# In a unit the next batch's values are projected ahead of the first value products, keys and the seventh product for maxima behind them

## The reference

```
x   = x + tanh(g_xattn) * Attention(layernorm(x), ctx)      # x [8, 56, 128], ctx [8, 1500, 128]
      q = xn @ w_q.T, k = ctx @ w_k.T, v = ctx @ w_v.T      # 16 heads of 8
      softmax(q k^T / sqrt(8)) v, then @ w_o.T
x   = x + tanh(g_ffn) * MoE(layernorm(x))                   # 8 experts, the best 2 of each token
```

## Time and profile before

| | us |
|---|---|
| median of three runs | 282.74 (282.09 to 285.79) |
| the profiled execution's own time | 280.42 |
| its span, from first to last instruction | 278.7 |
| PE busy | 265.4 (95%) |
| DVE busy | 216.7 (78%) |
| ACT busy | 178.6 (64%) |
| POOL busy | 125.2 (45%) |
| granted TensorE clock, mean | 0.999 |

### The profile page before, as it was taken

One profiled execution on the slowest core, in us unless ns is written; L12 is line 12 of the kernel. 1 busy time (PEld: TensorE's weight loads), 2 busy tenths in 40 slices (PEclk: granted clock), 3 DMA queues, 4 the chain that ended last, 5 costly groups with the idle time before them and its releaser, 6 DMA issues.

```text
span 278.7 us, 8055 instructions
## 1 busy us (share of the span) xinstructions
PE 265.4 (95%) x2807; PEld 218.9 (79%) x2807; DVE 216.7 (78%) x460; ACT 178.6 (64%) x369; POOL 125.2 (45%) x148
## 2 busy tenths in 40 slices
PE   7889899999999999999999999996989999999994
PEld 2466688888788888888878887885888789999962
DVE  4679788887977889788887887788466988888771
ACT  2637586687676777678668774465718878776500
POOL 3587852763466266195266310123520855554200
PEclk9999999999999999999999999999999999999999
DMA  7398964972990892695497299300000000000001
GB/s 256 102 205 215 215 154 118 255 187 57 245 237 23 239 240 75 171 238 145 109 243 202 53 214 284 125 0 2 2 2 1 0 0 0 0 5 0 0 0 33
DMA packets 9957, 32.40 MB, mean 116 GB/s; under 512 B 2592, under 2 KB 3104, under 8 KB 9920
## 3 DMA queue, kind: packets, MB, share of 16 engines
q1 hardware_dynamic: 9504, 31.80, 45.0%
q10 hardware_dynamic: 432, 0.33, 0.4%
HBM read 13.26 MB, written 0.23 MB: 48 GB/s over the span
## 4 chain that ended last, share of the span: by engine, by line
PE 74%; ACT 6%; DVE 6%; DMA 6%; SPq 3%; issue 2%; POOL 2%; DVEq 0%; ACTq 0%
PE max_ps L1053 14%; PE o_ps L1074 13%; PE score_ps L1033 13%; PE misc_ps L1012 7%; PE misc_ps L1005 5%; DMA ctx_sb<-in_ctxT 5%; SPq L251 3%; PE score_ps L1269 3%; ACT probs L548 3%; PE score_ps L1271 2%; PE score_ps L1270 2%; PE o_ps L1371 2%; PE o_ps L1269 2%; PE o_ps L1271 2%; PE o_ps L1270 2%
## 5 line engine op out<-in xcount | busy, mean ns | idle before, releaser
L734 DVE TENSOR_REDUCE part_max<-max_ps 112x1 f32<-112x512 f32 (+1 forms) x192 | 117.7, 666 | 28.6 <-PE max_ps L1053 26.8
L548 ACT ACTIVATE probs<-score_ps 128x448 f32<-128x448 f32 x188 | 88.0, 549 | 11.3 <-PE score_ps L1033 11.0
L1053 PE MATMUL max_ps<-kx,qx 96*112 96x512 f32 (+1 forms) x192 | 79.9, 422 | 2.3 <-DVE part_max L734 1.3
L1033 PEld LDWEIGHTS score_ps<-qx,kx 104*128 104x128 f32 x376 | 64.0, 188 | 7.8 <-issue 0.3
L1033 PE MATMUL score_ps<-qx,kx 104*128 104x224 f32 x376 | 67.3, 277 | 0.0
L1074 PE MATMUL o_ps<-probs,v_sb 128*32 128x112 f32 (+1 forms) x1536 | 45.2, 261 | 1.3 <-ACT probs L548 0.8
L1074 PEld LDWEIGHTS o_ps<-probs,v_sb 128*32 128x32 f32 (+1 forms) x1536 | 37.5, 110 | 7.5 <-ACT probs L548 5.1
L1053 PEld LDWEIGHTS max_ps<-kx,qx 96*112 96x112 f32 x192 | 33.7, 177 | 8.3 <-issue 4.6
L542 ACT ACTIVATE v_sb<-misc_ps 128x512 f32<-128x512 f32 x24 | 14.4, 601 | 29.2 <-PE misc_ps L1012 29.2
L370 POOL TENSOR_TENSOR k_low<-k_full,k_high 128x512 fp32r<-128x512 f32 (+1 forms) x21 | 26.3, 1252 | 13.8 <-ACT k_full L530 13.5
L406 POOL CAST ctx_parts<-ctx_sb 128x512 fp32r<-128x512 f32 (+1 forms) x18 | 10.8, 600 | 46.3 <-DMA ctx_sb<-in_ctxT 29.9
(11 more groups left out here) (192 smaller groups left out, 385.4 us busy)
## 6 DMA issues: line engine op xcount, KB each, us to landing
kx<-k_high SPq DMA_DIRECT2D x60, 187.5 KB, 5.3
kx<-k_low SPq DMA_DIRECT2D x30, 187.5 KB, 5.2
ctx_sb<-in_ctxT SPq DMA_DIRECT2D x7, 750.0 KB, 5.8
gu_sb<-in_guT SPq DMA_DIRECT2D x8, 512.0 KB, 5.5
dn_sb<-in_dnT SPq DMA_DIRECT2D x8, 256.0 KB, 5.8
ctx_sb<-in_ctxT SPq DMA_DIRECT2D x2, 256.0 KB, 3.9
kx<-k_high SPq DMA_DIRECT2D x4, 123.5 KB, 2.3
kx<-k_high SPq DMA_DIRECT2D x4, 64.0 KB, 2.0
```

Source lines behind the costliest of these rows:

```text
L548: nc.scalar.activation(probs[:, (KT * h + t) % 8, :], bank[:, 0:SC // 2], ACT.Exp, scale=SCALE).then_inc(exp_done, 1)
L734: nc.vector.reduce_max(part_max[:, p, c:c + 1], max_ps[0:PC, bank, 0:size], AX.X).then_inc(max_taken, turns)
L1033: last = nc.tensor.matmul(bank[0:m, GC * g:GC * g + GC], kx[0:KR, 2 * par + h, g, 128 * t:128 * t + m], qx[0:KR, par, 2 * h + g, :], start ...
L1053: nc.tensor.matmul(max_ps[0:PC, bank, 0:size], qx[0:MR, par, 2 * h + p // 2, PC * (p % 2):PC * (p % 2) + PC], kx[0:MR, slot, p // 2, start ...
```

## The change

Jobs 0 and 1 trade their kinds: job 0 becomes the values job and job 1 the keys job, in the loop's twelve units. The seventh product moves from in front of run 0 to behind it, in the fourteen units that share this code. ACT's order of copies follows. On DVE the wait for the reciprocals' completion moves in front of reductions 4 and 5, and the shuffle in front of the seventh reduction. The jobs at c = 2 stay.

```diff
             def evacuate(i, par, h, c):
                 b = batch(i, par)
-                if c == 1:
+                if c == 0:
                     v_copy(b + 1, 1 - par, 1 + h)
                 elif h == 1 and c == 2:
                     ...
                 else:
-                    if h == 0 and c == 0:
+                    if h == 0 and c == 1:
                         keys_moved(i, par)
                         act.wait_ge(k_low_saved, NCH * (b + 2))
-                    k_copy(b + 2, par, 2 if h else c // 2, misc_ps)
+                    k_copy(b + 2, par, 2 if h else c - 1, misc_ps)
...
                 reciprocals(u - 1, 1 - h)
+                dve.wait_ge(den_taken, u + 1)
                 for n in range(MID, RUN):
                     take_max(ring(u, n), n % 3, AHEAD + n)
-                dve.wait_ge(den_taken, u + 1)
+                spread_inverse(u - 1, 1 - h)
                 take_max(ring(u, SEVENTH), SEVENTH % 3, AHEAD + RUN, turns=2)
-                spread_inverse(u - 1, 1 - h)
...
             def project(i, par, h, c):
-                if h == 0 and c == 0:
-                    pe.wait_ge(v_saved, NCH * (b + 1) + 1)
-                    k_product3(i, par, 0)
+                if c == 0:
+                    if h == 0:
+                        pe.wait_ge(v_saved, NCH * (b + 1) + 1)
+                    else:
+                        pe.wait_ge(k_saved, 2 * (NCH * (b + 2) + 2))
+                    v_project(1 - par, 1 + h)
                 elif c == 1:
-                    pe.wait_ge(k_saved, 2 * (NCH * (b + 2) + 1 + 2 * h))
-                    v_project(1 - par, 1 + h)
+                    pe.wait_ge(v_saved, NCH * (b + 1) + 2 + h)
+                    k_product3(i, par, 2 * h)
                 elif h == 0:
-                    pe.wait_ge(v_saved, NCH * (b + 1) + 2)
+                    pe.wait_ge(k_saved, 2 * (NCH * (b + 2) + 1))
                     k_product3(i, par, 1)
-                elif c == 0:
-                    pe.wait_ge(k_saved, 2 * (NCH * (b + 2) + 2))
-                    k_product3(i, par, 2)
                 else:
-                    pe.wait_ge(v_saved, NCH * (b + 2))
+                    pe.wait_ge(k_saved, 2 * (NCH * (b + 2) + 3))
                     v_project(par, 0)
...
                 job(i, par, h, 0)
+                attend(i, par, h, 0)
                 max_scores(*u1, AHEAD + RUN, ring(u, SEVENTH), SEVENTH % 3, turns=2)
-                attend(i, par, h, 0)
                 job(i, par, h, 1)
```

## The result

| | before | after |
|---|---|---|
| median of 6 runs, us | 283.14 (282.09 to 285.79) | 288.03 (287.80 to 288.72) |
| the profiled execution's own time | 280.42 | 287.91 |
| its span | 278.7 | 286.2 |
| PE busy | 265.4 | 272.9 |
| DVE busy | 216.7 | 231.1 |

A forecast was written before the change was run, and what follows sets the result against it. The prediction took PE's order as the bound, with ACT's copy of job 1 and exponentials 6 to 8 in each unit's chain. ACT's copies +4.5 and the late context -2.5 gave +2.0 us: 284.7 from 282.74, range 279.9 to 288.3.

The forecast's parts named there:

- Run 0's start: On PE, with a values job alone in front, run 0 starts 0.07 (h = 0) and 0.11 us (h = 1) earlier.
- The credit of 0.18 a pair: The earlier starts of run 0 on PE, 0.07 us in h = 0 and 0.11 in h = 1, counted against the loss.
- ACT's copies: Behind job 1 one ACT copy becomes two; exponential 6 comes 0.45 (h = 0) and 0.30 us (h = 1) later, 4.5 in all.
- The doubt that I took from the Trainium skill: Shown matmul ends are computed, so PE's credits could be void: loss 5.7 us, forecast 1.2 higher; the credits were kept.
- The late context: In units of h = 0, ACT's waits for keys 0 caused by a late context go: a gain of 2.5 us.
- DVE: The wait for the reciprocals' completion in front of reductions 4 and 5 costs some 0.15 us a unit, taken as 0.
- this sign of being wrong: A new idle piece, POOL or DVE as releaser, in front of keys 1, product 10 or the transposed maxima.
- POOL: Chunk 1's split, released by keys 0, ends 0.75 us before keys 1 needs it, so it costs 0.
- The POOL rival: Slower case: chunk 1's split becomes the wait; 287.8 us, or 289.0 with the copies' loss at its upper bound; chance 0.10.
- SP: Chunk 2's `k_low` and twelve queued keys transfers come some 1.4 us later, the context goes out 2.3 earlier; cost 0.
- Absorbed: Faster rival: tile 11 does not carry the later exponentials to run 1, only the gain stays, 280.2 us; chance 0.17.

The follow-up runs named there:

- `k_low` late: Changed kernel with POOL's `k_low` of chunk 0 moved behind chunk 2's split; median 285.97 us, 1.0117 of the kernel before.
- run 1: No follow-up run: a step of PE in each unit, behind run 0, job 2 and the transposed maxima; 5.76 and 5.94 us behind run 0 in the kernel before.
- The extra copy: Kernel before with one more ACT copy of 128x512, into values not in use, in front of job 1's own; 287.79 us, ratio 1.0205.
- `k_low` held: Kernel before with POOL's `k_low` of chunk 0 waiting for scores tile 8 of h = 0; 286.46 us, ratio 1.0125.

## Why the prediction was right in sign and short in size

**Run 0's start: wrong, the first of the two steps that failed.** "Run 0 starts 0.07 and 0.11 earlier" rested on PE's own order: less stands in front, so it starts sooner. It starts 3.77 and 3.89 behind the output copy, where it had 3.77 and 3.81. I had looked at exponential 5 and not at the reciprocals, although L1063 waits for them and the earlier trace rows has them ending at 98.01 + 0.85 = 98.86, only 0.18 ahead of run 0 at 99.04. In after it is 0.20 and 0.24 behind them. The front of before was balanced: the product used PE time in which run 0 waited for DVE anyway. The credit of 0.18 a pair (1.1 in all) was none. The pair with `k_low` late, free of the part of DVE's hold that reached run 1, is 0.95 over before (23.39 - 22.44), and 0.75 + 0.18 = 0.93 is what the loss comes to without the credit.

**ACT's copies: right in mechanism and size.** Measured from run 0, exponential 6 moved by 0.50 and 0.39 to 0.40; my working says 0.98 - 0.49 + 0.03 = 0.52 and 0.92 - 0.50 - 0.02 = 0.40 (job 1's end behind run 0 is 0.03 later and 0.02 earlier by the working). With `k_low` late, run 1 is 0.52 and 0.40 later behind run 0 than in before (6.28 and 6.34). The extra copy confirms that such a shift reaches the end of the unit. The doubt that I took from the Trainium skill (Perfetto Trace Analysis, section on the Tensor Engine instruction), that the shown end of a matmul is computed, did not bear here, as far as this trace shows: the sizes came out as worked from those ends, and the credit was void for a cause of the kernel's own.

**The late context: right.** 2.5 forecast, 2.3 found in the lengths of units of the one trace of before, and the wait of 29.9 is 0.5.

**DVE: wrong, the larger failed step.** "I take 0" looked at the wait for the reciprocals, whose cover did hold (DVE still waits 0.17 for product 10). What cost time was a thing I had not asked: what POOL does while DVE makes the negated maxima. The split of chunk 1 begins 6.30 us behind the output copy (103.72 - 97.42) and not 3.63 (98.90 - 95.27), `k_low` follows it, and both now lie over DVE's small operations, which last until POOL's instruction ends. My own numbers held this: the prediction has the split from 101.52 to 103.48 with `k_low` behind it, and the two operations of before run from 103.24 to 103.60. It let `k_low` pass because nobody needs its result soon. From there: the three reductions start at 107.09, the transposed maxima at 107.83 and run 1 at 107.93, 6.74 behind run 0 where the kernel with `k_low` late has 6.29. 0.44 a pair, 2.6 us over six pairs. The prediction named this sign of being wrong, a new idle piece with DVE as releaser in front of the transposed maxima, and it is there, 0.32 us at 107.83.

**POOL: right for the wrong question.** Its split had the margin that I gave and a little more (it ends at 105.70, and keys 1 runs at 106.63 without waiting for it). The POOL rival did not come; POOL's cost came by way of DVE. The upper end of my range stood on that rival (287.8 and 288.3), so that 288.03 lies inside it is luck.

**SP: 0 held, with a wrong size.** Chunk 2's `k_low` starts 7.45 behind the output copy (116.88 - 109.43) where it was 4.64 (111.02 - 106.38), 2.8 later and not 1.4. The units' lengths, accounted for above, show no price for it.

**The sum** by measured terms: 4.5 + 1.1 (credit void) + 2.6 (DVE) - 2.3 = 5.9, against 6.06 in the traces. "Absorbed" fell: wherever exponential 6 came later than in before, run 1 came later by as much, within 0.01, or more. It does not hold the other way: with job 1 behind tile 7 exponential 6 is 0.94 earlier (2.04 behind run 0) and run 1 is not.

## What to carry to other kernels

Before work is moved away from in front of a step, list every wait of that step in the code and put the end of each beside its start: here one ended 0.18 to 0.24 us ahead of run 0, so emptying the front gained nothing, and the work cost 0.22 us a unit in its new place. When a change shifts another engine's schedule, lay that engine's long instructions over the short serial chains (here three DVE operations of 0.17 us) that the critical step waits for. A change made of several trades is worth taking apart: here the trade in h = 1 alone, with the second copy moved, gave the gain and none of the loss (pair 22.43, no late context behind unit 0).

## What the runs showed of the hardware

DVE operations of 0.16 to 0.17 us that read and write only SBUF took up to 1.20 us while POOL ran a 128x512 subtraction, and each ended within 0.03 us of POOL's end (105.73 and 105.70; 106.96 and 106.95; with `k_low` held, 108.98 and 108.95). The reduction of 12 numbers (L740), with a single SBUF input, kept its mean of 166 ns in both kernels, also in unit 6 of after, where it ran at 105.22 under POOL's split. The Trainium skill (SBUF — State Buffer, section "Who interferes with whom") says that DVE and GpSimd share a pair of ports under an exclusive lock that the first holder keeps for its whole instruction, that a cast or a DVE operation with two SBUF inputs can need it and a reduction does not. The traces agree, down to which operations are held.
